# Selective scan of a Mamba layer: ten of sixteen input products made by ScalarE on a transposed dt*x and transposed into PSUM by TensorE

## The reference, cut to what matters

```python
dbl = xc @ x_w.T
dt, Bm, Cm = jnp.split(dbl, [DT_RANK, DT_RANK + D_STATE], axis=-1)
dt = jax.nn.softplus(dt @ dt_w.T + dt_b)
A = -jnp.exp(A_log)
dA = jnp.exp(dt[..., None] * A)
dBx = dt[..., None] * Bm[:, :, None, :] * xc[..., None]
def step(h, inp):
    dA_t, dBx_t, C_t = inp
    h = dA_t * h + dBx_t
    y = jnp.einsum('bds,bs->bd', h, C_t)
    return (h, y)
```

## Time and profile before

| | |
|---|---|
| median of three runs | 2965.06 us |
| the profiled execution | 2967.89 us, its span 2966.1 us |
| busy in the span | PE 84%, DVE 78%, POOL 70%, ACT 53% |
| mean granted clock of PE | 0.899 of full speed |
| forward and backward scan in the span | about 880 to 1714 us, and 1760 to 2690 us |

### The profile page before, as it was taken

The page is one execution under the profiler, slowest core; times in us unless marked ns, Lnnn a source line. Parts: engine busy times, 40 slices in busy tenths (PEclk is TensorE's granted clock), DMA queues, the critical chain, the costliest instruction groups (busy, mean ns, idle before and its releaser), DMA issues. The chain is left out here.

```text
span 2966.1 us, 34800 instructions
## 1 busy us (share of the span) xinstructions
PE 2497.7 (84%) x7800; PEld 1190.2 (40%) x7800; DVE 2318.3 (78%) x2487; ACT 1576.8 (53%) x2784; POOL 2084.2 (70%) x1166
## 2 busy tenths in 40 slices
PE   7899999957468988889889858899889889988598
PEld 7666666624322323323323223333333333336422
DVE  4366666560659999999999939998999899895499
ACT  6466666543655655555656446555555555545221
POOL 3133333230359999999999949999999999995155
PEclk6699999969779999999999889999999999997599
DMA  3000000000256777777777637776766676660022
GB/s 60 8 9 9 9 9 9 6 1 0 59 167 223 243 244 237 247 235 240 246 236 241 227 124 235 219 236 216 229 226 222 221 225 224 218 211 17 13 54 47
DMA packets 177295, 437.72 MB, mean 148 GB/s; under 512 B 65638, under 2 KB 70219, under 8 KB 177228
## 3 DMA queue, kind: packets, MB, share of 16 engines
q1 hardware_dynamic: 139340, 420.19, 44.5%
q10 hardware_dynamic: 37888, 16.79, 2.1%
HBM read 404.40 MB, written 24.12 MB: 144 GB/s over the span
## 5 line engine op out<-in xcount | busy, mean ns | idle before, releaser
L1443 POOL TENSOR_TENSOR sb_hc<-sb_h,sb_cc 128x1024 f32<-128x1024 f32 x256 | 599.7, 2360 | 61.8 <-PE sb_py L1232 56.2
L1443 POOL TENSOR_TENSOR sf_hc<-sf_h,sf_cc 128x1024 f32<-128x1024 f32 x256 | 595.8, 2347 | 11.5 <-DVE sf_h L1521 8.2
L1232 PE MATMUL sf_py<-sf_hc,ident 128*128 128x512 f32 x1024 | 533.1, 655 | 0.6 <-POOL sf_hc L1443 0.6
L1232 PE MATMUL sb_py<-sb_hc,ident 128*128 128x512 f32 x1024 | 519.5, 638 | 0.0
L572 POOL TENSOR_TENSOR ar_sc<-ar_sc,ar_mx 128x512 f32<-128x512 f32 x128 | 154.7, 1208 | 356.6 <-DVE ar_mx L513 356.6
L1521 DVE TENSOR_TENSOR_SCAN sf_h<-sf_dA,sf_state,sf_pu 128x1024 f32<-128x1024 f32 x160 | 375.4, 2346 | 19.1
L1521 DVE TENSOR_TENSOR_SCAN sb_h<-sb_dA,sb_state,sb_pu 128x1024 f32<-128x1024 f32 x160 | 375.2, 2345 | 17.1
L1232 PEld LDWEIGHTS sf_py<-sf_hc,ident 128*128 128x128 f32 x1024 | 197.0, 205 | 269.3 <-issue 239.8
L1232 PEld LDWEIGHTS sb_py<-sb_hc,ident 128*128 128x128 f32 x1024 | 187.3, 196 | 241.0 <-issue 232.0
L1501 DVE TENSOR_TENSOR sb_pu<-sb_pu,sb_dtx 128x1024 f32<-128x1024 f32 x160 | 193.9, 1212 | 52.7 <-PE sb_pu L1212 52.7
L1436 POOL TENSOR_TENSOR sb_dbx<-sb_dtx,sb_bb 128x1024 f32<-128x1024 f32 x96 | 226.5, 2359 | 3.3 <-DVE sb_dtx L1482 3.3
(11 more groups left out here) (294 smaller groups left out, 4594.6 us busy)
## 6 DMA issues: line engine op xcount, KB each, us to landing
sf_cc<-rows_scratch SPq DMA_DIRECT2D x256, 512.0 KB, 4.4
sb_cc<-rows_scratch SPq DMA_DIRECT2D x256, 512.0 KB, 4.4
sf_bb<-rows_scratch SPq DMA_DIRECT2D x96, 512.0 KB, 5.4
...
```

Of the source, the lines that this page charges most:

```text
L1232: ins = nc.tensor.matmul(p_y[:, hf], lhsT=c.ident[:, :], rhs=hc[:, s % RING, hf], start=False, stop=(s == U - 1))
L1443: nc.gpsimd.tensor_tensor(hc[:, s % RING, :], h[:, s % RING, :], cc[:, s % C_RING, :], ALU.mult).then_inc(read, 1)
```

## The change

The tables of the states change. `BY_G` is gone: POOL makes no input product, and SP loads no broadcast rows of B. DVE keeps six of the ten products it had (`BY_V`); ten go to ACT (`BY_A`). All sixteen decays go to the SBUF ring `dA`, now of 4 instead of 5 tiles.

For a state of `BY_A` the product is made with the tokens on the partitions. Once for a chunk PE multiplies eight blocks of xc by the B weights, which gives B with tokens on the partitions (`columns_b`; ACT copies it to `bT`), and transposes `dtx` in eight blocks (`turn_x`; ACT copies it to `dtxT`). For each such state ACT runs eight activations of 128 x 128, `Copy` with a scale that is a column of `bT` (`scale`, tile `sT`, a ring of two), and PE transposes the eight blocks back into `p_u[s % 2]` (`turn_in`), where the scan reads them. `keep` now copies two states at a time.

```diff
-C_RING, B_RING, DECAY_RING = 4, 3, 5
-DECAY_AHEAD, INJECT_AHEAD, LAG_SUM = 3, 2, 4
-BY_G = (2, 5, 7, 10, 13, 15)
-BY_V = tuple(s for s in range(16) if s not in BY_G)
+C_RING, DECAY_RING, TURN_RING = 4, 4, 2
+DECAY_AHEAD, SCALE_AHEAD, LAG_SUM = 3, 3, 4
+BY_V = (0, 1, 4, 6, 8, 14)
+BY_A = (2, 3, 5, 7, 9, 10, 11, 12, 13, 15)
...
+            def columns_b(m, par):
+                pe.wait_ge(r_copied, m + 1)
+                for j in range(BLOCKS):
+                    ins = nc.tensor.matmul(p_p[:, j * STATES:(j + 1) * STATES], lhsT=xc[:, par, j * Q:(j + 1) * Q],
+                                           rhs=k["bc"][:, 0:STATES], start=True, stop=True)
+                ins.then_inc(bt_made, 1)
+            def turn_x(m, par):
+                pe.wait_ge(dtx_done, m + 1)
+                for j in range(BLOCKS):
+                    ins = nc.tensor.transpose(p_p[:, j * Q:(j + 1) * Q], dtx[:, par, j * Q:(j + 1) * Q], c.ident[:, :])
+                ins.then_inc(x_turned, 1)
+            def turn_in(n, par, s):
+                r = BY_A.index(s)
+                pe.wait_ge(scaled, n * NA + r + 1)
+                need(pe, scanned, n * U + s - 1)
+                for j in range(BLOCKS):
+                    ins = nc.tensor.transpose(p_u[s % 2][:, j * Q:(j + 1) * Q], sT[:, (par * NA + r) % TURN_RING, j, :], c.ident[:, :])
+                ins.then_inc(turned_in, 1)
...
             prepare = [(0, convolve(a)), (0, convolve(b)), (2, in_out(a)), (3, in_out(b)),
-                       (5, step_size(a)), (6, step_size(b))]
+                       (4, columns_b), (6, step_size(a)), (6, step_size(b)), (13, turn_x)]
             if back:
-                run(pe, unit, prepare, [(13, project)], [(4, gate_in(a)), (4, gate_in(b))])
+                run(pe, unit, prepare, [(14, project)], [(5, gate_in(a)), (5, gate_in(b))])
...
+            def take_columns_b(m, par):
+                act.wait_ge(bt_made, m + 1)
+                nc.scalar.copy(bT[:, par, :, :].rearrange("p j s -> p (j s)"), p_p[:, 0:BLOCKS * STATES]).then_inc(bt_taken, 1)
+            def take_turned_x(m, par):
+                act.wait_ge(x_turned, m + 1)
+                need(act, scaled, NA * m)
+                nc.scalar.copy(dtxT[:, :, :].rearrange("p j d -> p (j d)"), p_p[:, :]).then_inc(xt_taken, 1)
+            def scale(n, par, s):
+                r = BY_A.index(s)
+                if r == 0:
+                    act.wait_ge(bt_taken, n + 1)
+                    act.wait_ge(xt_taken, n + 1)
+                need(act, turned_in, n * NA + r + 1 - TURN_RING)
+                for j in range(BLOCKS):
+                    ins = nc.scalar.activation(sT[:, (par * NA + r) % TURN_RING, j, :], dtxT[:, j, :], ACT.Copy,
+                                               scale=bT[:, par, j, s:s + 1])
+                ins.then_inc(scaled, 1)
...
             def keep(n, s):
-                act.wait_ge(scanned, n * U + s + 1)
+                act.wait_ge(scanned, n * U + s + 2)
                 e = 0 if back else TC - 1
-                nc.scalar.copy(state[:, s:s + 1], h[:, s % RING, e:e + 1]).then_inc(kept, 1)
+                nc.scalar.copy(state[:, s:s + 2], h[:, s % RING:s % RING + 2, e]).then_inc(kept, 1)
...
-            prepare = [(1, silu_x), (4, bc_rows), (5, load_flat), (6, part_high), (7, softplus_relu), (7, softplus_abs),
-                       (8, softplus_exp), (8, softplus_one), (8, softplus_log), (9, part_middle), (11, store_parts),
-                       (11, take_dt), (12, load_parts)]
+            prepare = [(1, silu_x), (4, bc_rows), (5, load_flat), (5, take_columns_b), (6, part_high), (7, softplus_relu),
+                       (7, softplus_abs), (8, softplus_exp), (8, softplus_one), (8, softplus_log), (9, part_middle),
+                       (11, take_dt), (12, store_parts), (14, take_turned_x), (14, load_parts)]
```

More of the change, by code:

```diff
@@ L1111, in scan_direction @@
             sem(s) for s in ("r_copied", "r_stored", "f_loaded", "high", "remained", "middle", "lowest", "p_stored"))
+        bt_made, bt_taken, x_turned, xt_taken, scaled, turned_in = (
+            sem(s) for s in ("bt_made", "bt_taken", "x_turned", "xt_taken", "scaled", "turned_in"))
         p_loaded = [sem("p_loaded%d" % j) for j in range(2)]
@@ L1114, in scan_direction @@
         c_spread = [sem("c_spread%d" % j) for j in range(C_RING)]
-        b_spread = [sem("b_spread%d" % j) for j in range(B_RING)]
         block = ctx.enter_context(nc.Block())
@@ L1127, in past @@
         def past(order, n, s, ring):
-            r = order.index(s) - ring
-            return n * U + order[r] + 1 if r >= 0 else (n - 1) * U + order[r + len(order)] + 1
+            r = order.index(s)
+            if r >= ring:
+                return n * U + order[r - ring] + 1
+            return (n - 1) * U + order[max(q for q in range(len(order)) if q % ring == r % ring)] + 1
         def run(eng, unit, prepare=(), tail=(), own=()):
@@ L1175, in step @@
                     pe.wait_ge(n_loaded[par], 16 * (m + 2 - par))
[L1176 to L1177 removed]
+                    need(pe, xt_taken, m)
                     if back:
@@ L1255, in unit @@
                     spread_b(m, mpar, ms)
+                if ms in BY_A and not (last and s == U - 1):
+                    turn_in(m, mpar, ms)
                 if s >= LAG_SUM:
@@ L1446, in unit @@
             def unit(n, par, s, first, last):
-                if first and s == 0:
-                    for j in range(INJECT_AHEAD):
-                        if j in BY_G:
-                            inject(0, 0, j)
-                m, mpar, ms = after(n, par, s + INJECT_AHEAD)
-                if ms in BY_G and not (last and s + INJECT_AHEAD >= U):
-                    inject(m, mpar, ms)
                 if s:
@@ L1528, in _ @@
             run(dve, unit, [(9, lost), (10, step_sum), (12, dt_x)],
-                [(LAG_SUM - 1, gate), (14, add_x)] if back else [])
+                [(LAG_SUM - 1, gate), (15, add_x)] if back else [])
             if back:
@@ L1577, in chunk @@
                         load_y(n + 1)
-                    m, _, ms = after(n, 0, s + 4)
-                    if ms in BY_G and m < NC:
-                        spread_b(m, ms)
                     spread_c(n, s)
@@ L1587, in _ @@
                 load_y(0)
-            for s in range(4):
-                if s in BY_G:
-                    spread_b(0, s)
             chunk(0, first=True)
```

93 lines of the change are left out of this document (37 added, 56 removed).

## The result

The changed kernel takes 3199.33 us (median; 3192.96 to 3210.01) against 2964.85 us for the kernel before on the same chips: ratio 1.0801, 95% interval 1.0764 to 1.0837. It is 8% slower, some 235 us. The forecast was 3137, in a range of 3000 to 3260.

The account below looks back on a forecast made before the run. ACT's list was taken to bound the changed kernel, with chunks of 60.6 us forward and 62.5 backward. Forward 90, backward 64 and edges 18 made +172 us on 2965, so 3137 us, range 3000 to 3260.

Parts of the forecast that it names:

- (a): ACT's wait from the `bc_rows` store until it landed and `load_flat` can issue: 3.7 us, of which 2.2 stay uncovered.
- (b): ACT's wait from `load_flat` to the cast that needs it: 5.2 us, of which 1.2 stay uncovered.
- (c): ACT's wait from `store_parts` to `load_parts`: 5.4 us, of which 1.9 stay uncovered.
- I take 1.2 in all.: ACT's other forward waits per chunk: decay for scan 0 (0.2 to 0.6 us), `silu_x` and `take_y` (about 1 together).
- Edges: First and last chunks of each direction, outside the 14 intervals: net +9 us per direction, 18 in all.
- ACT-bound: Main case: ACT's list bounds chunks of 60.6 us forward and 62.5 backward, 3137 us in all; chance 0.72.
- the first case: ACT's list bounds the chunk as worked out; own range 3043 to 3230 us; chance 0.72.
- the second: Column operand nearly free in ACT's short activations, so PE decides: about 2995 to 3010 us; chance 0.08.
- Faster by a lighter list: ACT's blocks take at most 0.18 us each, DVE becomes the bound and the kernel is faster: 2803 us; chance 0.10.
- a column that is nearly free: Scale column costs almost nothing in ACT's short activations; PE decides, about 2995 to 3010 us; chance 0.08.
- No overlap between blocks: ACT's 80 blocks per chunk do not overlap: 7.2 us more per chunk, 3340 us in all; chance 0.05.
- The low clock: PE's transposes don't keep its clock up: 7 to 8 us more per chunk, about 3350 us; chance 0.05.

Follow-up runs that it names:

- loads-by-SP run: Changed kernel with the two loads that wait for a DMA landing (flat and bcs) issued by SP in place of ACT: 1.0732 of the kernel before.
- copy-first run: Changed kernel with ACT copying the last state columns ahead of its unit's decay and block set, not behind them: 1.0480 of the kernel before.
- each edit alone: Changed kernel with one of: constant activation scale (1.0528), state copy first (1.0480), sum over states from bf16 products with C (1.0494); ratios to the kernel before.
- the three together: Changed kernel with state copy first, constant activation scale and the sum over states from bf16 products with C: 0.9839 of the kernel before (2915 us).

## Why the prediction was right, and where not

- *Sign and size.* Right: 172 us forecast, 232 in the profile (90 forecast and 110 measured in the forward window, 64 and 97 in the backward one).
- *ACT's list.* Forecast 54.8 us busy forward and 55.7 backward (56.4 and 57.3 less the 1.6 of DMA issues); measured 54.6 and 55.8. A block: 0.29 forecast, 0.304 measured; the rows of longer instructions carried over to a short one.
- *DMA waits and issues.* 3.0 us of waits forecast at three places; measured forward 30.1/14 = 2.2, all at (a), while (b) and (c) cost ACT nothing, and backward none. The 1.6 us of issues were put on ACT's list in full; the waits show at most 0.6 of them outside the wait at (a) (8.2/14, the decay behind the copy of the B rows). The loads-by-SP run shows that even these waits were worth less than they look.
- *"I take 1.2 in all."* This is the mis-sized term. ACT's waits forward without the DMA of (a) and its own copy of the B rows are 64.5 us, 4.6 per chunk, nearly half of them decays that wait for a scan (30.4). The forecast counted the wait of the decay for scan 0 and that of silu, but not that the scan of an even state waits for a copy that is queued behind a block set, although the order of ACT shows it (L1418 behind L1377). The copy-first run gave 2.0 us per chunk forward and 3.1 backward back. Backward ACT is idle for 9.1 us of a chunk, against 6.8 forecast (1.6 + 3 + 2.2); the largest wait there, 2.8 us, is the one for `columns_b` that the forecast named.
- *Luck.* The forward chunk is only 1.5 us off because two errors point opposite ways: DMA waits and issues came out 1.9 us lower than forecast, the other waits 3.4 higher.
- *PE.* Forecast between 52 and 57.8 forward, 57.5 and 62.4 backward; measured 54.6 and 60.0. "Close behind ACT forward" was right; backward PE is above ACT (60.0 against 55.8), and PE is one of three that count, which the forecast carried only as 2.2 us backward. Chunks: 60.6 forecast and 62.1 measured, 62.5 and 64.8.
- *POOL and DVE.* 41 and 47.7 forecast, 40.9 and 47.5 measured. DVE waits above all for the spreads (72.2 us of the forward window), the state copy (67.0) and the softplus (38.2), less for `turned_in` (20.5) and not for `dA`, the two that the forecast named. POOL waits for PE's sums (234.2) and hardly for DVE (12.1). The decays in SBUF, put at nothing, cost nothing here; on the kernel before they cost 319 us.
- *Edges.* 18 forecast, 25 measured.
- *"ACT-bound".* Too strong a word. Taking 7.2 us off ACT's list gave 2.3 to 2.6. Three limits lie close behind each other, ACT's list, PE's list and the order of the state copy: each edit alone gives back 81 to 95 us, and the three together 285. In which units of a chunk each of them binds was not worked out beyond the one stretch shown.
- *Sums.* By its own terms the low end of the first case is 2965 + 14 x 3.3 + 14 x 1.6 + 18 = 3052, not 3043, and the low end of the second, 2995, lies outside the stated range.
- *The rivals.* Faster by a lighter list, and a column that is nearly free: the price per block decided against both. No overlap between blocks: they overlap, 0.304 us each at a duration of 0.389. The low clock: it comes once per chunk, forward after the 6.28 us of idle time, and is gone before the sum of the next unit (1153.43 to 1155.31, 1.88 us for four); the granted clock of the window is 0.94 as before.
